# Windowed attention with a feed-forward pipeline on one core: query product ahead of the key sums, scores one position earlier

## What is computed

```python
qkv = x @ Wqkv                                # 16 heads of 64
q = l2norm(q) * qs; k = l2norm(k) * ksc       # per head and token
q, k = rotated(q), rotated(k)                 # products with cos and sin tables
sim = einsum('bhwie,bhwje->bhwij', bq, look(bk)) * 8    # windows of 32 look at 64 keys
out = einsum('bhwij,bhwje->bhwie', softmax(where(mask, -big, sim)), look(bv))
x = out @ Wo + x
x = (a * gelu(gate)) @ W2 + b2 + x            # from layernorm(x) @ W1 + b1
```

## Time and profile before

| | us |
|---|---|
| median of 3 runs | 2035.12 (2031.43 to 2035.75) |
| the profiled execution | 2030.68 |
| its span | 2028.9 |
| PE matmul, busy | 1800.8 (89%) |
| DVE, busy | 1529.0 (75%) |
| ACT, busy | 1380.8 (68%) |
| POOL, busy | 1262.7 (62%) |
| mean granted TensorE clock | 0.963 of 2.4 GHz |

### The profile page before, as it was taken

The page is one execution under the profiler, slowest core; times in us unless marked ns, Lnnn a source line. Parts: engine busy times, 40 slices in busy tenths (PEclk is TensorE's granted clock), DMA queues, the critical chain, the costliest instruction groups (busy, mean ns, idle before and its releaser), DMA issues. The chain is left out here.

```text
span 2028.9 us, 59338 instructions
## 1 busy us (share of the span) xinstructions
PE 1800.8 (89%) x24192; PEld 992.7 (49%) x24192; DVE 1529.0 (75%) x2543; ACT 1380.8 (68%) x2862; POOL 1262.7 (62%) x1127
## 2 busy tenths in 40 slices
PE   5898898668899999899999999999999999999984
PEld 3443444524555555455555555555555555555541
DVE  4778886247878788687878888878888788877753
ACT  1454455337787777787778877888778877778752
POOL 4303200058877777677777787777877778777721
PEclk8999999769999999999999999999999999999996
DMA  8000000225333343333433335333353333333310
GB/s 183 13 2 1 2 2 2 63 47 100 74 71 80 79 88 75 68 69 69 85 84 86 69 71 93 82 78 69 78 92 84 70 69 77 69 79 78 69 22 21
DMA packets 136894, 132.61 MB, mean 65 GB/s; under 512 B 79016, under 2 KB 82664, under 8 KB 136296
## 3 DMA queue, kind: packets, MB, share of 16 engines
q1 hardware_dynamic: 136624, 128.81, 29.8%
HBM read 20.94 MB, written 1.05 MB: 11 GB/s over the span
## 5 line engine op out<-in xcount | busy, mean ns | idle before, releaser
L1000 ACT ACTIVATE prob<-s_in,lower,rq 128x64 f32<-128x64 f32 x1536 | 537.7, 429 | 94.5 <-POOL lower L1109 94.2
L861 PE MATMUL bank_a<-x_shift,wqk_sb 128*128 128x512 f32 x768 | 377.5, 615 | 79.4 <-ACT sq L1030 68.2
L880 PE MATMUL bank_y<-zT,wvo 128*128 128x512 f32 x768 | 345.5, 593 | 0.0
L1089 POOL TENSOR_TENSOR sumk<-sq 128x512 f32<-128x512 f32 x96 | 122.3, 1274 | 254.8 <-ACT sq L1030 254.8
L861 PEld LDWEIGHTS bank_a<-x_shift,wqk_sb 128*128 128x128 f32 x768 | 141.7, 195 | 273.3 <-issue 151.4
L880 PEld LDWEIGHTS bank_y<-zT,wvo 128*128 128x128 f32 x768 | 146.1, 190 | 184.3 <-issue 184.3
L382 ACT ACTIVATE a_prob<-a_sT 128x1024 f32<-128x1024 f32 x128 | 130.5, 1023 | 104.4 <-PE a_sT L216 102.5
L491 DVE TENSOR_REDUCE a_negmax<-a_max 128x1 f32<-128x512 f32 x256 | 164.6, 685 | 46.9 <-PE a_max L166 43.1
L996 ACT ACTIVATE zT<-bank_z 128x1024 f32<-128x1024 f32 x192 | 186.1, 1022 | 10.3 <-PE bank_z L872 7.7
L1077 POOL TENSOR_TENSOR prob<-prob,rden 128x1024 f32<-128x1024 f32 x96 | 182.9, 1905 | 3.9 <-DVE rden L1183 3.9
L894 PEld LDWEIGHTS bank_z<-kpad,qpair 64*32 64x32 f32 x12288 | 129.7, 105 | 107.5 <-issue 107.3
(11 more groups left out here) (161 smaller groups left out, 3947.0 us busy)
## 6 DMA issues: line engine op xcount, KB each, us to landing
qpair<-qfin SPq DMA_DIRECT2D x384, 128.0 KB, 2.4
kpad<-kfin SPq DMA_DIRECT2D x384, 128.0 KB, 2.4
wqk_sb<-in_wqkv SPq DMA_DIRECT2D x24, 256.0 KB, 5.6
xk_prev<-xk_own SPq DMA_DIRECT2D x24, 192.0 KB, 2.5
ffn_sb<-in_ffn SPq DMA_DIRECT2D x6, 537.5 KB, 3.7
wv_in<-in_wqkv SPq DMA_DIRECT2D x12, 256.0 KB, 4.6
wo_in<-in_wo SPq DMA_DIRECT2D x6, 512.0 KB, 6.0
xk_prev<-xk_own SPq DMA_DIRECT2D x24, 48.0 KB, 2.1
```

The costliest lines, as they stand in the source:

```text
L861: last = pe.matmul(bank_a[:, half, :], wqk_sb[:, layer_of(u) % 2, part, half, g * P:(g + 1) * P], cols(u), start=True, stop=True)
L880: last = pe.matmul(bank_y[:].rearrange("p (t w q) -> p t w q", w=WPT, q=WIN), wvo[:, layer_of(u), GH * g + 2 * (hh % 2) + hh // 2, :], zT[ ...
L1000: last = act.activation(prob[:, n % 2, i, :], s_in[:, n % 2, i, :], ACT.Exp, bias=lower[:, n % 2, i:i + 1], scale=rq[:, n % 2, i:i + 1])
L1089: pool.tensor_tensor(sumk[:], sq[:, 0, :], sq[:, 1, :], ALU.add).then_inc(sumk_ok, 1)
```

## The change

The same operations are done, in another order and with other waits. The main moves: PE takes projecting out in two parts (three heads behind the key product, the fourth behind weighing), the query sums of c and the scores of c come ahead of the query product of n, and the key sums right behind that product. On ACT there are two orders, one for steps with gelus; in the other, `exponentials` come in groups of 2, 4, 6 and 4, the query factor of c between the two query squares, the key factor behind them and ahead of the last four `exponentials`, and the two copies of zT are apart, upper half first. DVE sums the weights at the start of the step (e instead of d), takes the mask ahead of the query products and the row maximum between them. On POOL `lower` moves ahead of the query sums; the keys are joined in kfin and multiplied there. The feed-forward weights get two buffers, and the projection weights of the next layer are loaded in eight pieces over eight steps. The order of ACT before stands in the code above; the gelu step's later part, which has `exponentials` in groups of 9, 2 and 5, is left out here.

```diff
-                layer, left = divmod(s - 4 * B - LAG_FF - 2, 16)
+                layer, left = divmod(s - 4 - OUTPUT, 16)
                 if left == 0 and 0 <= layer < DEPTH - 1:
-                    after(sp, xf_ok, B * layer + B - 1)
-                    sp.dma_start(ffn_sb[:], ffn[layer + 1]).then_inc(ffn_loaded, 16)
+                    after(sp, xf_ok, B * layer - 1)
+                    sp.dma_start(ffn_sb[:, (layer + 1) % 2], ffn[layer + 1]).then_inc(ffn_loaded, 16)
                 if quarter(n):
                     after(sp, s_mm, n - 1)
...
-                if left == 2 and layer + 1 < DEPTH:
+                if 2 <= left < 10 and layer + 1 < DEPTH:
                     after(sp, q_mm, 16 * layer - 1)
-                    load_projection(layer + 1)
+                    load_projection(layer + 1, left - 2)
...
-                    project_out(h)
+                    project_out(h, 0, 3)
+                for stage, ok in ((GATE, gelu_ok), (LINEAR, hid_ok)):
+                    v = unit_at(s - 1, stage)
+                    if v is not None:
+                        after(pe, ok, v)
+                if quarter(c):
+                    after(pe, sumq_ok, c)
+                    after(pe, floor_ok, c)
+                    for t in range(TPB):
+                        last = pe.matmul(bank_f[:, 0:TPB * GH].rearrange("q (e t p) -> q t e p", e=2, t=TPB)[:, t],
+                                         sumq[:, t * P:(t + 1) * P], pick_head[:],
+                                         start=True, stop=True, skip_group_check=True)
+                    last.then_inc(sumq_mm, 1)
+                    after(pe, kpad_in, c, 64)
+                    after(pe, qpair_in, c, 64)
+                    after(pe, z01_ok, e - 1)
+                    scores(c)
                 if quarter(n):
                     after(pe, sqk_ok, n)
                     after(pe, pk_ok, n)
                     project(n, 0, q_mm)
-                for stage, back, ok in ((2, 0, xn_ok), (2, 1, xnT_ok), (3, 1, gelu_ok), (4, 1, hid_ok), (5, 1, xf_ok)):
+                    after(pe, sumk_ok, n)
+                    after(pe, floorq_ok, c)
+                    pe.matmul(bank_f[:], same_head[:], sumk[:], start=True, stop=True).then_inc(sumk_mm, 1)
+                for stage, back, ok in ((NORM, 0, xn_ok), (NORM, 1, xnT_ok), (GATE, LINEAR - GATE, gelu_ok), (LINEAR, 1, hid_ok),
+                                        (OUTPUT, 1, xf_ok)):
                     v = unit_at(s - back, stage)
                     if v is not None:
                         after(pe, ok, v)
...
                     after(pe, xk_ok, rows_at(s - 1))
                 if quarter(e):
                     after(pe, pT_ok, e)
-                    after(pe, mask_ok, min(c - 1, QUARTERS - 1))
+                    after(pe, mask_ok, min(c, QUARTERS - 1))
                     after(pe, xk_ok, e // GROUPS)
                     after(pe, prev_in, e // GROUPS, 32)
                     weigh_rows(e)
...
+                if quarter(h):
+                    project_out(h, 3, 4).then_inc(y_mm, 1)
                 if quarter(e):
                     after(pe, z23_ok, e)
...
+                    if quarter(n):
+                        after(act, k_mm, n)
+                        after(act, sumq_ok, n - 1)
+                        act.activation(sq[:, 0, :], bank_a[:, 0, :], ACT.Square).then_inc(sqk0_ok, 1)
+                        after(act, pk2_ok, n)
+                        act.activation(sq[:, 1, :], bank_a[:, 1, :], ACT.Square).then_inc(sqk_ok, 1)
...
+                else:
+                    if quarter(d):
+                        after(act, lower_ok, d)
+                        after(act, pT_ok, d - 2)
+                        after(act, den_ok, d - 2)
+                        exponentials(d, 0, 2)
+                    if quarter(n):
+                        after(act, k_mm, n)
+                        after(act, sumq_ok, n - 1)
+                        act.activation(sq[:, 0, :], bank_a[:, 0, :], ACT.Square).then_inc(sqk0_ok, 1)
+                    if quarter(d):
+                        exponentials(d, 2, 6)
+                    if quarter(n):
+                        after(act, pk2_ok, n)
+                        act.activation(sq[:, 1, :], bank_a[:, 1, :], ACT.Square).then_inc(sqk_ok, 1)
+                    u_own = rows_at(c)
+                    if u_own is not None:
+                        after(act, xk_mm, u_own)
+                        after(act, z_mm, 4 * (u_own - 2) + 3)
+                        copy(xk_own[:, u_own % 2].rearrange("p t c -> p (t c)"), bank_z[:, 2, :]).then_inc(xk_ok, 1)
+                    u_turned = unit_at(c, NORM)
+                    if u_turned is not None:
+                        after(act, ffn_loaded, layer_of(u_turned), 16)
+                        after(act, xnT_mm, u_turned)
+                        after(act, lin_mm, u_turned - 1)
+                        act.activation(xnT[:], bank_z[:, 3, :], ACT.Identity, bias=ff_column(u_turned, 2 * FCH + 2), scale=ff_column(u_turned, 2 * FCH + 1)).then_inc(xnT_ok, 1)
+                    if quarter(d):
+                        exponentials(d, 6, 12)
+                    if quarter(n):
+                        after(act, q_mm, n)
+                        after(act, sumk_ok, n)
+                        act.activation(sq[:, 0, :], bank_a[:, 0, :], ACT.Square).then_inc(sqq0_ok, 1)
+                    if quarter(c):
+                        after(act, floorq_ok, c)
+                        after(act, lower_ok, c - 2)
+                        act.activation(rq[:, c % 2], rq_sum[:], ACT.Ln).then_inc(lnq_ok, 1)
+                        after(act, lnq_ok, c)
+                        act.activation(rq[:, c % 2], rq[:, c % 2], ACT.Exp, bias=log8[:], scale=-0.5).then_inc(rq_ok, 1)
+                    if quarter(n):
+                        after(act, pq2_ok, n)
+                        act.activation(sq[:, 1, :], bank_a[:, 1, :], ACT.Square).then_inc(sqq_ok, 1)
+                    if quarter(e):
+                        after(act, z_mm, e)
+                        after(act, y_mm, e - 2)
+                        z = zT[:, e % 2].rearrange("p w t h q -> p w (t h q)")
+                        copy(z[:, 2:4, :], bank_z[:, 2:4, :]).then_inc(z23_ok, 1)
+                    if quarter(n):
+                        after(act, floor_ok, n)
+                        act.activation(rk[:], rk[:], ACT.Ln).then_inc(lnk_ok, 1)
+                        after(act, lnk_ok, n)
+                        act.activation(rk[:], rk[:], ACT.Exp, scale=-0.5).then_inc(rk_ok, 1)
+                    if quarter(d):
+                        exponentials(d, 12, 16).then_inc(exp_ok, 1)
+                    if quarter(e):
+                        after(act, z_mm, e)
+                        after(act, y_mm, e - 2)
+                        z = zT[:, e % 2].rearrange("p w t h q -> p w (t h q)")
+                        copy(z[:, 0:2, :], bank_z[:, 0:2, :]).then_inc(z01_ok, 1)
 
...
                     after(pool, pk_ok, n)
-                    pool.tensor_tensor(pk[:, 0, :], pk[:, 0, :], pk[:, 1, :], ALU.subtract)
-                    pool.tensor_tensor(pk[:, 2, :], pk[:, 2, :], pk[:, 3, :], ALU.add).then_inc(rotk_ok, 1)
+                    after(pool, kpad_in, n - 1, 64)
+                    pool.tensor_tensor(kfin[:, 0, :], pk[:, 0, :], pk[:, 1, :], ALU.subtract)
+                    pool.tensor_tensor(kfin[:, 1, :], pk[:, 2, :], pk[:, 3, :], ALU.add).then_inc(rotk_ok, 1)
+                if quarter(c):
+                    after(pool, max_ok, c)
+                    after(pool, rq_ok, c)
+                    after(pool, exp_ok, c - 2)
+                    pool.tensor_tensor(lower[:, c % 2], s_max[:], rq[:, c % 2], ALU.mult).then_inc(lower_ok, 1)
+                if quarter(n):
                     after(pool, sqq_ok, n)
                     after(pool, sumq_mm, n - 1)
                     pool.tensor_tensor(sumq[:], sq[:, 0, :], sq[:, 1, :], ALU.add).then_inc(sumq_ok, 1)
...
                     pool.tensor_tensor(qfin[:, 1, :], pq[:, 2, :], pq[:, 3, :], ALU.add).then_inc(qfin_ok, 1)
                     after(pool, rk_ok, n)
                     after(pool, rotk_ok, n)
-                    after(pool, kpad_in, n - 1, 64)
-                    pool.tensor_tensor(kfin[:, 0, :], rk[:], pk[:, 0, :], ALU.mult).then_inc(kfin0_ok, 1)
-                    pool.tensor_tensor(kfin[:, 1, :], rk[:], pk[:, 2, :], ALU.mult).then_inc(kfin_ok, 1)
-                if quarter(c):
-                    after(pool, max_ok, c)
-                    after(pool, rq_ok, c)
-                    after(pool, exp_ok, c - 2)
-                    pool.tensor_tensor(lower[:, c % 2], s_max[:], rq[:, c % 2], ALU.mult).then_inc(lower_ok, 1)
+                    pool.tensor_tensor(kfin[:, 0, :], rk[:], kfin[:, 0, :], ALU.mult).then_inc(kfin0_ok, 1)
+                    pool.tensor_tensor(kfin[:, 1, :], rk[:], kfin[:, 1, :], ALU.mult).then_inc(kfin_ok, 1)
 
...
+                if quarter(e):
```

(23 more changed lines are left out.)

192 lines of the change are left out of this document (74 added, 118 removed).

## The result

| | before | after |
|---|---|---|
| median, us | 2035.43 (2031.43 to 2036.29) | 2087.71 (2086.32 to 2092.08) |
| ratio to before, 95% interval | | 1.027 (1.025 to 1.029) |
| span of the profiled execution | 2028.9 | 2086.5 |
| mean granted TensorE clock | 0.963 | 0.956 |

The change costs 2.7%. It was forecast as slower, at 2064 with 2042 to 2088 for the rival that carried the forecast; it is slower by 52 us where 29 was forecast, and lies 0.3 us inside the upper end of those bounds. Three places of the page after tell most of it: PE's share, the wait ahead of the scores, and the wait of `lower` on GpSimd. Columns of the groups: busy us and mean ns, then idle us before them and what ended it.

A forecast was written before the change was run, and what follows sets the result against it. PE was taken to bound the kernel, with small holes; after the edit a loop between engines would set the steps. Units +21, first steps +5, end -3, clock +8 gave +31, 2062; 2 added made 2064 us (2042 to 2088).

The forecast's parts named there:

- the rival that carried the forecast: Slower because the loop between engines sets the step: 2042 to 2088 us, chance 0.55.
- The ring: Query product, vector products, maximum, GpSimd, key transfer, scores, next query product: each of 96 steps at least 15.6 us (15.3 to 15.9).
- Norm to gate: Step from norm to gate stage: VectorE's residual, sum, products, xn and mask start the ring 0.8 us late, 16.4 us.
- linear to output: Step from linear to output stage: PE's path through projecting out, linear, keys, query sums and scores takes 15.7 us.
- Gate to linear: Step from gate to linear stage: PE waits for the gelus ahead of the query sums, 15.8 us.
- The norm step: Output to norm takes 15.85 us; VectorE's work from residual to mask makes the ring start 0.8 us late.
- The loads: Split weight loads, doubled feed-forward buffer and eight pieces: no wait of PE for them, so 0.
- First steps: First eight steps, without feed-forward work, at 15.6 us each: 124.8 against 120.2, +5 us (0 to +12).
- the rival on the clock: Clock drops in nearly all norm steps and the first eight, 1.9 us each there: 2090 to 2110 us, chance 0.17.
- The clock: Holes of 2.4 us before z[0:2] in norm steps, half followed by a drop to 1.2 GHz: +8 us (0 to +30).
- The end: Scores of the last quarter don't wait for anything of PE: -3 us (-6 to +3).
- The regular term: Units of four steps take 63.8 us against 62.8, +1.0 each over 21.5 units: +21 us.

The follow-up runs named there:

- run 4: Kernel after with only `lower` moved behind the `kfin` products on GpSimd, the maximum left between the vector products; 2079.06 us, ratio 1.022.
- Runs 1: Kernel after with one more 1.27 us addition on GpSimd just ahead of the query sum, written to an unused tile; 2217.55 us, ratio 1.091.
- 2: Kernel after with the same addition on GpSimd, but in its idle time ahead of `lower`; 2088.57 us, ratio 1.027.
- Runs 6: Kernel after with the sum of the weights in norm steps taken over 12 of 64 columns on the vector engine; 2076.84 us, ratio 1.020.
- 9: `max_late` with the last feed-forward addition moved behind the next step's weight sum and reciprocal, the last unit's addition left out; 2017.80 us, ratio 0.991.
- 10: `max_late` with run 9's edit, and xn made on ScalarE by scale and shift, last unit's addition still left out; 2004.41 us, ratio 0.985.
- Run 5: Kernel before with only the change's loads: two feed-forward buffers and projection weights in eight pieces over eight steps; 2032.61 us, ratio 1.000.
- max_late: Kernel after with the row maximum behind the query products and the floor, `lower` last on GpSimd; 2030.50 us, ratio 0.999.
- norm_light_full: `max_late` with the feed-forward addition behind the next weight sum and xn made on ScalarE, last unit's addition included; 2008.61 us, ratio 0.987.
- sum_last: `norm_light_full` with the query sum moved last on GpSimd; 1975.90 us, ratio 0.971.
- run 12: The kernel `sum_last`: `norm_light_full` with the query sum moved last on GpSimd; 1975.90 us, ratio 0.971.
- run 3: The kernel `max_late`: kernel after with the row maximum behind the query products and the floor, `lower` last on GpSimd; 2030.50 us, ratio 0.999.
- run 11: The kernel `norm_light_full`: `max_late` with the feed-forward addition behind the next weight sum, xn on ScalarE, last unit's addition included; 2008.61 us, ratio 0.987.
- run 8: `max_late` with the mask behind the second query products on the vector engine, TensorE keeping the scores first; 2205.86 us, ratio 1.083.

## Why the prediction was right and where it was short

**The ring: right, term by term.** The forecast had 15.6 us. Measured in the turn shown: query start to maximum 1.32 (forecast 1.33), maximum to `lower` 1.29 (1.30), `lower` 0.18 (0.17), query sum to last `kfin` 4.89 (4.94), last `kfin` to scores 4.45 (4.40 and a wait of 0.1), scores 1.50 (1.40 and a wait of 0.1), query product to query start 2.02 (1.92); sum 15.65. Norm to gate, 15.65, and linear to output, 15.57, have the wait for the keys in them. Gate to linear, 15.63, comes out at the same length by the other path that the forecast gave for it, the gelus ahead of the query sums (15.8): TensorE waits there for the gelus, and run 4 leaves it unchanged. Runs 1 and 2 show the ring by intervention: 1.27 us more cost a step 1.2 us in the ring and nothing beside it. Two signs of the forecast came weaker than said: the wait ahead of the scores in 56 of 96 steps, and the little spread, since 37.5 us of extra stand against 21.6 before. That the query product no longer waits for the key squares, and that the gain goes into the ring, came as said: the gelu step won 2.03 us and the unit lost 0.7 on balance (forecast 1.0; linear to output came 0.1 and gate to linear 0.2 under it).

**The norm step: right.** The forecast's 15.85 for the interval into it plus a vector engine 0.8 late is 16.65; measured 16.64. Runs 6, 9 and 10 each take work off that engine ahead of the norm step's query start and move this interval alone. The exact agreement is in part luck: with the lateness gone the interval is 15.64, so by these runs the 15.85 was 0.2 too long and the lateness 1.0, not 0.8.

**The loads: right as far as it was tried.** Run 5 gives 1.000 for them, under the old cover.

**First steps: the term was too small.** Forecast +5 for eight steps; the first 12 intervals cost +19.2, and the first eight of them lasted 17.2 in the mean, not 15.6. The step of the working that failed is that the ring was summed with durations at full clock, while the granted clock between 420 and 620 us was 0.93 before and fell to 0.90 after: products and scores that lie in the ring take longer at 1.2 GHz, and nothing covers them. The second interval shows it (timelines of PE and DVE):

```profile
448.70 2.05 PE L899 MATMUL bank_z<-kpad,qpair 64*32 64x64 f32 x128 [5.39 <-DMA kpad<-kfin]
450.68 3.24 PE L866 MATMUL bank_a<-x_shift,wqk_sb 128*128 128x512 f32 x4
...
453.96 0.75 DVE L1202 SCALAR_TENSOR_TENSOR pq<-bank_a,scale_sb,rot_sb 128x512 f32<-128x512 f32 x1 [1.88 <-PE bank_a L866]
```

Scores to product take 1.98 where the full clock gives 1.50, product to query start 3.28 where it gives 2.02: 1.74 more, and with the ring's 15.65 that is 17.39. The interval lasted 17.40. In the first three of these steps, where neither weighing nor projecting out has begun, TensorE waits 4.3 to 5.5 us for the keys. Two late landings (in intervals 5 and 9) come on top. I had the slow products in the rival on the clock, at 1.9 a step for the first eight, and that price was about right. `max_late` took 11.7 of the 19.2 back.

**The clock: the sign was right, the mechanism wrong.** I put +8 on a hole of 2.4 us in each norm step, where projecting out waits for z[0:2]. The hole is there, but with 1.3 to 1.6 us from 620 us on, and the matmuls right behind it run at full speed:

```profile
1232.66 2.84 PE L885 MATMUL bank_y<-zT,wvo 128*128 128x512 f32 x6 [1.59 <-ACT zT L1009]
```

The drops, seven in 83 steps at +2.6 to +3.2, stand at the end of the scores' wait for a late key transfer; so do the four of `max_late` and the three of `norm_light_full`, and `sum_last`, without late landings there, has none. The length of the wait doesn't sort them: one of 1.36 us was followed by slow matmuls, one of 2.26 us wasn't (the query products at 1730.77 and 1893.09):

```profile
1729.05 1.79 PE L899 MATMUL bank_z<-kpad,qpair 64*32 64x64 f32 x128 [1.36 <-DMA kpad<-kfin]
1730.77 3.20 PE L866 MATMUL bank_a<-x_shift,wqk_sb 128*128 128x512 f32 x4
...
1891.68 1.48 PE L899 MATMUL bank_z<-kpad,qpair 64*32 64x64 f32 x128 [2.26 <-DMA kpad<-kfin]
1893.09 1.99 PE L866 MATMUL bank_a<-x_shift,wqk_sb 128*128 128x512 f32 x4
```

The granted clock was 0.57 over 1729.8 to 1733.8 and 1.00 over 1891 to 1896. In the forecast, "steps that are long for other reasons are taken to stay as they are" is the step that failed: extra went from 21.6 to 37.5. The working counted the transfer at its median of 2.4 us; while 6.9 us covered it, a landing at 4 would have cost nothing. Without cover the rare late one counts in full, and the clock adds to it. The rule of the Trainium skill (TensorE: Matmul & The Clock Gate, "Why this matters for your kernels"), to keep gaps between bursts under about 3 us, would call both waits of 1.99 and 2.20 harmless; the trace differs, with a granted clock of 0.57 right behind the wait of 1.99 us.

**The end: wrong sign.** Forecast -3, measured +9.2. In `max_late` the end is 109.5, so it isn't the maximum; in `norm_light_full` it is 104.6, so about half of the loss goes with the norm step's vector work. The forecast looked at the last scores alone, and these do end 2.7 us sooner (13.8 us behind the last query start, 16.5 before). But the last `exponentials` end 12.9 us later (37.8 against 24.9). Before, the last quarter's 16 ran in one group; after, ScalarE's order puts a copy of zT ahead of the last four, and that copy waits for the weighing of another quarter (timeline of ACT after):

```profile
1998.19 4.08 ACT L1013 ACTIVATE prob<-s_in,lower,rq 128x64 f32<-128x64 f32 x12
2011.28 1.02 ACT L1009 ACTIVATE zT<-bank_z 128x1024 f32<-128x1024 f32 x1 [9.01 <-PE bank_z L877]
2012.20 1.42 ACT L1013 ACTIVATE prob<-s_in,lower,rq 128x64 f32<-128x64 f32 x4
```

In a step of the middle the same copy waits 0.84 us (1179.36). No run changed this order by itself.

**The sum.** Forecast +31 on the profiled run; measured +57.6: regular +14.2 (forecast +21.5), first steps +19.2 (+5), extra +15.9 (+8), end +9.2 (-3), start -1.1. The regular term is counted over fewer steps here, 83 rather than 21.5 units. The terms mis-sized are those of the first steps, of the extra and of the end: a ring summed at full clock, a landing counted at its median, and an end judged by its scores alone. The +8 for holes that cost no clock stood in for half of the extra, which is luck.

**Left open.** That the fetches delay the transfers rests on the order of the packets, which wait for the end of the fetch in every late case that has one among the last piece's packets; it wasn't tried by moving a fetch alone. That the late landings then cause the drops of the clock is by their order in the trace, and why some long waits aren't followed by a drop stays open. In run 12 the missing late landings and the shorter ring come together, so what each is worth in the 14.5 us of extra isn't told apart.

## What to carry to other kernels

When an operand crosses four engines and a transfer before the next step may start, write down that ring and add it up before moving the consumer earlier: the consumer's place decides whether the transfer has cover, and no engine's busy share shows it. Then look for what stands on the ring without belonging to it. Here a maximum, its scaling and a sum stood there. Taking out the first two won back the whole 2.7% (run 3), and the sum won 1.6% more (run 12); the rest of the way to -2.9% came from lightening the vector engine in the norm step (runs 9 to 11). The order on TensorE stayed the same throughout. A move that fills one hole (the mask, in run 8) can close a second ring over another engine's order, so follow each moved instruction's consumers for one whole step.

## What the runs showed of the hardware

- An instruction fetch of 16 KB (0.9 to 1.4 us) among the packets of a 128 KB transfer from SBUF to SBUF held back its last four packets of 2 KB until the fetch was over, and the transfer landed after 3.5 to 4.2 us instead of 2.4. Of the 15 quarters with a late piece 14 were the same in `max_late`, a kernel of equal instruction count, so this tail isn't chance.
- A wait of TensorE of 1.99 us was followed by about 3.4 us at 1.2 GHz (granted clock 0.57 over 651 to 655); the waits of 1.3 to 1.6 us for z, one in each unit, were not. Length alone doesn't sort them: a wait for the keys of 1.36 us (1729.05) was followed by slow matmuls, one of 2.26 us (1891.68) wasn't.
- Four activations on ScalarE of 128x128 that read PSUM, with scale and bias of their own for each partition, took 35.7 us for 96, 0.37 each, with 452 ns from start to end of one (I had put 0.3), by the groups of `norm_light_full`:

```profile
L1107 ACT ACTIVATE xn<-bank_z,shift,rstd 128x128 f32<-128x128 f32 x96 | 35.7, 452 | 10.8 <-POOL shift L1166 10.8
```
